# Cross-attention scores: four 32x128 products replaced by sixteen 32x32 products in a post-LN decoder layer on one core

## What is computed

```
x = layernorm(x + self_attention(x))          # linear attention, no softmax
q = x @ W_q.T + b_q ; k, v = from the context # 16 heads of 32 features
scores = q . k / sqrt(32)                     # per head: 2048 x 154, contraction over 32
attn   = softmax(where(mask == 0, -1e9, scores))
x = layernorm(x + (attn @ v) @ W_o.T + b_o)
r = sigmoid(xr @ W_r.T) ; k = relu(xk @ W_k.T) ** 2
x = layernorm(x + r * (k @ W_v.T))            # xr, xk mix x with the previous token
```

## Time and profile before

| | |
|---|---|
| median of three runs | 918.7 us |
| span of the profiled execution, first to last instruction | 916.3 us |
| PE (matmul) busy | 903.6 us, 99% |
| PEld (weight load) busy | 735.5 us, 80% |
| DVE / ACT / POOL busy | 715.3 / 552.3 / 507.2 us |
| instructions in the trace | 19,065, of them 6,726 matmuls and 6,726 weight loads |

### The profile page before, as it was taken

The page is one execution under the profiler, slowest core; times in us unless marked ns, Lnnn a source line. Parts: engine busy times, 40 slices in busy tenths (PEclk is TensorE's granted clock), DMA queues, the critical chain, the costliest instruction groups (busy, mean ns, idle before and its releaser), DMA issues.

```text
span 916.3 us, 19065 instructions
## 1 busy us (share of the span) xinstructions
PE 903.6 (99%) x6726; PEld 735.5 (80%) x6726; DVE 715.3 (78%) x1994; ACT 552.3 (60%) x1667; POOL 507.2 (55%) x505
## 2 busy tenths in 40 slices
PE   8999999999999999999999999999999999999997
PEld 7867767777888888887878888888787878787876
DVE  7697566577887878797979788887878787879775
ACT  7455236857765656565757575756665757575631
POOL 1053015858684757575756657575666766656420
PEclk9999999999999999999999999999999999999999
DMA  8771020113010000002000000101010100100001
GB/s 300 240 248 49 27 91 9 35 43 127 9 47 9 30 26 24 31 24 89 24 31 24 31 24 24 31 25 31 24 30 25 31 25 14 41 2 24 2 24 46
DMA packets 31033, 45.65 MB, mean 50 GB/s; under 512 B 2779, under 2 KB 15579, under 8 KB 30811
## 3 DMA queue, kind: packets, MB, share of 16 engines
q1 hardware_dynamic: 27339, 37.36, 12.7%
q10 hardware_dynamic: 3600, 7.08, 2.2%
HBM read 34.10 MB, written 9.70 MB: 48 GB/s over the span
## 4 chain that ended last, share of the span: by engine, by line
PE 75%; DVE 5%; issue 3%; POOL 3%; ACT 1%; POOLq 0%; ACTq 0%
PE dense L88 18%; PE dense L90 17%; PE dense L89 17%; PE turned L1590 5%; PE scores L1578 4%; PE rest_value L1604 4%; PE rest_value L1608 3%; PE dense L1477 2%; PE turned L1477 1%; PE rest_value L1596 1%; POOL row_inv L1383 1%; POOL prob L1389 1%; PE scores L1483 1%; DVE prob L1112 1%; DVE stats L1071 1%
## 5 line engine op out<-in xcount | busy, mean ns | idle before, releaser
L1383 POOL TENSOR_TENSOR row_inv<-row_sum,minus_one 128x4 f32<-128x4 f32 x128 | 145.9, 1139 | 255.1 <-ACT prob L794 253.5
L794 ACT ACTIVATE prob<-prob,row_min 128x154 f32<-128x154 f32 x512 | 209.5, 417 | 17.8 <-DVE row_min L1112 17.8
L1389 POOL TENSOR_TENSOR prob<-prob,row_inv 128x512 f32<-128x512 f32 x128 | 142.1, 1110 | 0.0
L1112 DVE CUSTOM_DVE_ANT_0 prob<-scores,mask_add 128x154 f32<-128x154 f32 x512 | 127.1, 310 | 3.7 <-PE scores L1578 3.7
L802 ACT ACTIVATE prob_t<-turned 128x512 f32<-128x512 f32 x128 | 75.9, 593 | 57.5 <-PE turned L1590 57.4
L794 ACT ACTIVATION_READ_ACCUMULATOR prob<-prob,row_min 128x1 f32 x512 | 98.7, 193 | 0.0
L1590 PE MATMUL turned<-ident,prob 128*128 128x128 f32 x512 | 77.0, 273 | 1.3 <-ACT prob_t L802 0.8
L88 PE MATMUL dense<-xt_hi,cross_wq_hi 128*128 128x256 f32 x256 | 75.0, 293 | 0.5 <-DVE xt_lo L1103 0.5
L88 PE MATMUL dense<-mix_k_hi,ffn_wk_hi 128*128 128x256 f32 x256 | 74.5, 291 | 0.0
L1170 DVE TENSOR_TENSOR k_act_lo<-square,k_act_hi 128x512 fp32r<-128x512 f32 x32 | 50.3, 1573 | 28.2 <-ACT k_act_hi L827 28.2
L89 PE MATMUL dense<-xt_lo,cross_wq_hi 128*128 128x256 f32 x256 | 72.2, 282 | 0.0
(11 more groups left out here) (296 smaller groups left out, 2709.4 us busy)
## 6 DMA issues: line engine op xcount, KB each, us to landing
x_rows<-x_rows SPq DMA_DIRECT2D x32, 256.0 KB, 3.6
xt_raw<-x_cols SPq DMA_DIRECT2D x16, 512.0 KB, 3.7
out<-gate_then_y SPq DMA_DIRECT2D x15, 512.0 KB, 2.8
mask_in<-mask SPq DMA_DIRECT2D x16, 154.0 KB, 2.4
cross_wv<-cross_wv SPq DMA_DIRECT2D x2, 512.0 KB, 5.9
cross_wk<-cross_wk SPq DMA_DIRECT2D x1, 1024.0 KB, 8.7
self_wv<-self_wv ACTq DMA_DIRECT2D x1, 1024.0 KB, 7.6
self_wk<-self_wk ACTq DMA_DIRECT2D x1, 1024.0 KB, 12.0
```

Of the source, the lines that this page charges most:

```text
L794: m = act.activation(keys, keys, ACT.Exp, bias=row_min[:, buf, t, h:h + 1], scale=-1.0, accum_out=row_sum[:, buf, t, h:h + 1])
L1112: m = dve.tensor_tensor_reduce(prob[buf][:, t, h * CTX:(h + 1) * CTX], s_bank[:, h, t * CTX:(t + 1) * CTX], mask_add[n % 2][:, t, :], -SCA ...
L1383: pool.tensor_tensor(row_inv[:, buf, t, :], row_sum[:, buf, t, :], minus_one[:], ALU.pow).then_inc(*p_inv.up)
L1389: pool.tensor_tensor(keys[:, :, 0:P], keys[:, :, 0:P], inv.broadcast_to([P, HPG, P]), ALU.mult).then_inc(*p_norm.up)
```

## The change

In `scores` each product of 128 tokens is cut into four of 32 tokens. Loop j runs over the quarters of a token tile; quarter j is written to the partitions 32j to 32j+31 of the same bank and columns as before. Contraction rows, keys, banks, waits, the final signal and every other engine's program stay as they are. A call issues 32 products where it issued 8.

```
+                b = batch(n)
                 for t in range(TPG):
-                    for h in range(HPG):
-                        rows, b = slice(h * DK, (h + 1) * DK), batch(n)
-                        m = pe.matmul(s_bank[:, h, t * CTX:(t + 1) * CTX], q[rows, g, t * P:(t + 1) * P],
-                                      kt[rows, g, b * CTX:(b + 1) * CTX], start=True, stop=True, skip_group_check=True)
+                    for j in range(P // DK):
+                        to, tokens = slice(j * DK, (j + 1) * DK), slice(t * P + j * DK, t * P + (j + 1) * DK)
+                        for h in range(HPG):
+                            rows = slice(h * DK, (h + 1) * DK)
+                            m = pe.matmul(s_bank[to, h, t * CTX:(t + 1) * CTX], q[rows, g, tokens],
+                                          kt[rows, g, b * CTX:(b + 1) * CTX], start=True, stop=True, skip_group_check=True)
                 m.then_inc(*s_mm.up)
```

## The result

The changed kernel takes 938.98 us (median of four runs, 938.57 to 939.14), the one before 918.6 in the same comparison: ratio 1.0223, 95% interval 1.0209 to 1.0238. It is slower by 20.4 us. The sign and the range of the prediction hold; the size does not: 5.4 us were forecast.

What follows compares the result with a forecast made beforehand. TensorE, its matmul side busy 99% of the span, was taken as the bound. Per call -0.080 + 0.18 = +0.10 us, taken as 0.085, times 64 gave +5.4 us: 924.1 us against 918.7, range 915 to 950.

Steps and rivals of the forecast that it cites:

- All on the path: Whole kernel: every microsecond a score burst gains or loses on TensorE moves the end; 64 x 0.085 = 5.4 us.
- Waves, nothing: Score burst: four waves of 0.131 us for each array tile stay, sixteen key streams running at an unchanged rate.
- Fill -0.080: Start of a score burst: loading 32 columns instead of 128 cuts the first matmul's excess from 0.105 to 0.025 us.
- Stagger +0.18: Start of a score burst: with loads taking turns, the sixteenth product starts at 0.20 us instead of 0.02; bounds +0.08 and +0.18.
- Instructions, 0 to +0.08, taken as 0: Score burst: 128 instructions a call instead of 32 arrive in time; late delivery costs 0 to 0.08 us, taken as 0.
- Emptying 0.08: End of a score burst: draining the array before the next form of product may load stays at 0.08 us.
- The rival with the shadow of the load: Between `values` and `scores`: new loads need not wait for the 0.08 us drain; burst 0.65 us, kernel 913.6 us; 18%.
- The rival with four at a time: Score burst: only four products run at once however small, +1.5 us a call, 1015 us; 6%.
- The rival with fewer than sixteen in flight: Score burst: TensorE looks ahead far enough for only eight products, +0.4 to +0.5 us a call, 945 to 951 us; 13%.
- the "no change" rival: Start of a score burst: second loads wait until all sixteen first ones are out; +0.08 cancels -0.08, 918.7 us; 16%.
- The rule that spoke for the other sign: Start of a score burst: 15 x 4 = 60 ns between first and last product, burst 0.69 us, -2.6 us in all.

Runs made afterwards that it cites:

- dup4: The kernel before with each 32x128 product of the scores issued twice for its token tile, same result: 949.68 us (ratio 1.0342).
- half4: The kernel before with the scores of token tile 0 only, four 32x128 products a call instead of eight: 907.2 us (ratio 0.9877).
- half16: The changed kernel with the scores of token tile 0 only, sixteen 32x32 products a call: 907.9 us (ratio 0.9884).
- jth: The changed kernel with the loops in the order quarter, token tile, head, same 32 products: 964.51 us (ratio 1.0504).
- rot: The changed kernel with the quarters of the second token tile in the order 2, 3, 0, 1: 939.13 us (ratio 1.0226).
- n12: The changed kernel without quarter 3 of both token tiles, 24 products a call: 930.91 us (ratio 1.0137).

## Why the prediction was off

The mechanism on which the sign rested (a shorter fill against a longer start, all on TensorE's path) is there, but it comes to almost nothing; the loss comes from a limit that I had among the rivals in another form.

- *All on the path*: right for a loss. 64 x 0.34 is the whole difference; dup4 confirms it with 31.4 of 33.5 us. For a large gain it is wrong: of half4's 17 us only 11.2 arrived.
- *Waves, nothing*: right. Sixteen streams run at the rate of four; the median matmul is 289 ns in both.
- *Fill -0.080*: right, 0.026 of excess instead of 0.105.
- *Stagger +0.18*: too large. The last of sixteen starts at 0.12, so the term is +0.10. I had loads take turns, 0.0067 us each; in fact thirty loads stand beside sixteen matmuls in the first 0.13 us, two to each start. The lower bound of +0.08 was nearly it. The two last starts come 0.016 us apart: after 56 instructions the queue has run out, and each product waits for its four. At 4 ns each some 25 of the 56 came during the burst, so about 30 stood ready at its start, an estimate.
- *Instructions, 0 to +0.08, taken as 0*: this is the step that failed. I asked whether instructions are delivered fast enough, and for an unbroken burst they are, at about 4 ns. I did not ask in this term how many can be open at once. Opening sixteen products with two passes each takes a window of 64, and a call needs 128. So the rest of the call is held outside the window, the array gets next to no new work from 0.27 to 0.47, and after that the delivery, harmless by itself, sets the pace at 0.016 us a product. The term is +0.33, nearly half of it that pace.
- *Emptying 0.08*: right. The last wave ends at 0.87 + 0.131 = 1.00 and the next product's load starts at 1.09 (331.76 - 330.67). The forecast for that load was 0.81.
- *The rival with the shadow of the load* (18%): did not come. The load side stands idle 0.41 us before the burst in both kernels.
- *The rival with four at a time* (6%): did not come. Sixteen start within 0.12 us.
- *The rival with fewer than sixteen in flight*: I set the limit on how many waiting second passes TensorE passes over, and it passes over fifteen. The limit lies on the instructions between the oldest unfinished and the newest, and it bites in the second token tile only. Its price (+0.4 to +0.5) was near because both stop the array for about as long, not because the mechanism was right. That 939 lies within the range is luck of the same kind, since the range was stretched upward for this rival.

With the two terms set right the sum is -0.08 + 0.10 + 0.33 = +0.35 us a call, 22 us; the chain shows 0.34. Without the window the change would be worth -0.08 + 0.10, a microsecond slower, the "no change" rival; half16 against half4 (+0.7 us, with one token tile a call) is the nearest case measured.

The rule that spoke for the other sign, 4 ns for each further tile (the Trainium skill, "TensorE: Matmul & The Clock Gate", section "Measured speedup vs the span model"), doesn't hold here: starts are 0.0067 us apart in every form that was run. The Trainium skill, "TensorE: Matmul & The Clock Gate", section "Step-by-step: what each phase is for", speaks of a 64-deep reorder window, and the stop at the 33rd matmul, the 66th instruction, agrees with that number. It adds that matmuls stay in program order among themselves. Here they don't, if a float32 product's second pass stands next to its first in the code: fifteen later products start in between.

## What to carry to other kernels

Before cutting a product into more array tiles, count the instructions of the burst in code order: a float32 product takes four (two loads, two matmuls), and once some 64 stand between the oldest unfinished one and the next, the array waits for the oldest to finish (a matmul lasts some 0.3 us here), not for free tiles. Put products of different array tiles next to each other, since two of one tile close together use up the window (jth, +25.5 us by order alone). Where all 128 columns are in use already, as here, cutting gained only part of the load at the start of a burst, and of the three forms run the middle one was best: 32x64, 1.6 us faster than 32x128 and 22 us faster than 32x32.

## What the runs showed of the hardware

- The 33rd matmul in code order starts 0.03 us after the first one has ended by the profile, in the changed kernel and in rot, and in n12 at the same 0.34 us. The product behind it starts at 0.48, 0.03 us after the second matmul has ended; its tile would let it start at 0.30. That time is also 0.131 us after the 33rd matmul, and no run separates the two. Whether the limit counts 64 instructions or 32 matmuls stays open, since every matmul here has its load. It doesn't count whole pairs: the 33rd load starts at 0.16 (0.21 in rot), before the first matmul has ended.
- TensorE starts matmuls of different array tiles past fifteen waiting second passes: sixteen that wait for their load (0.31 us) within 0.12 us, then sixteen of 0.289 from 0.156 on. If both passes of a product stand together in the code, that is out of code order.
- Starts are 0.0067 us apart for 32x128, 32x64 and 32x32 products alike while instructions stand ready, and two loads of 32 columns start in that time.
- Sixteen 32x32 products side by side each stream 154 keys in the 0.131 us that four 32x128 products take: the second pass starts that long after the first has its load, in both.
- Instructions came at about 4 ns each where none stood ready: a product of four each 0.016 us.
